# Another opening, and the weighted values of the second half one piece later, in a kernel of two cross-attention layers

## What is computed

```python
q = hidden_state @ Wq + bq                    # 112 x 512
k = encoder_hidden_state @ Wk + bk            # 375 x 128
v = encoder_hidden_state @ Wv + bv            # 375 x 128
...
scores = jnp.einsum('bkgld,bksd->bkgls', q, k) * scale
scores = scores + encoder_attention_mask[:, :, None, :, :]
attn = jax.nn.softmax(scores, axis=-1)
out = jnp.einsum('bkgls,bksd->bkgld', attn, v)
out = out.transpose(0, 3, 1, 2, 4).reshape(b, l, H)
out = out @ Wo + bo
x = out + hidden_state
...
return (x - mu) * jax.lax.rsqrt(var + EPS) * gamma + beta
```

## Time and profile before

| | |
|---|---|
| time before, median of 3 runs | 1741.35 us (1740.72 to 1744.32) |
| the profiled execution's own time | 1738.81 us |
| its span, from the first to the last instruction | 1737.0 us |
| PE busy | 1695.1 us, 98% of the span |
| DVE, ACT, POOL busy | 1267.2, 1042.3, 572.3 us |
| mean granted TensorE clock | 0.990 of full speed |

### The profile page before, as it was taken

The page is one execution under the profiler, slowest core; times in us unless marked ns, Lnnn a source line. Parts: engine busy times, 40 slices in busy tenths (PEclk is TensorE's granted clock), DMA queues, the critical chain, the costliest instruction groups (busy, mean ns, idle before and its releaser), DMA issues. The chain is left out here.

```text
span 1737.0 us, 35992 instructions
## 1 busy us (share of the span) xinstructions
PE 1695.1 (98%) x10881; PEld 1005.9 (58%) x10881; DVE 1267.2 (73%) x1713; ACT 1042.3 (60%) x2370; POOL 572.3 (33%) x1169
## 2 busy tenths in 40 slices
PE   5999999999999999999999999999999999999997
PEld 3555566665565665565665565655665655656652
DVE  5567777787777777777777776777767877767776
ACT  2556666666665656665656665666656666656564
POOL 3133332333332333332333323333323333323332
PEclk8899999999999999999999999999999999999999
DMA  8546555455545465555565454455454455453541
GB/s 283 146 121 170 147 122 143 128 145 143 147 120 142 124 151 145 135 130 147 128 156 145 114 136 130 118 135 145 105 135 125 128 138 139 109 135 115 139 113 55
DMA packets 288390, 235.83 MB, mean 136 GB/s; under 512 B 140858, under 2 KB 262964, under 8 KB 288084
## 3 DMA queue, kind: packets, MB, share of 16 engines
q1 hardware_dynamic: 266852, 204.14, 43.8%
q10 hardware_dynamic: 21488, 31.06, 7.3%
HBM read 101.39 MB, written 22.02 MB: 71 GB/s over the span
## 5 line engine op out<-in xcount | busy, mean ns | idle before, releaser
L922 DVE TENSOR_REDUCE mx<-ms 128x2 f32<-128x750 f32 x896 | 809.2, 924 | 399.0 <-PE ms L1090 392.5
L740 ACT ACTIVATE probs<-sc 125x448 f32<-125x448 f32 x1522 | 744.6, 542 | 281.8 <-PE sc L1061 274.7
L1090 PE MATMUL ms<-ks,qs 96*128 96x375 bf16 (+1 forms) x2560 | 443.0, 327 | 11.4 <-DVE mx L922 8.7
L1061 PE MATMUL sc<-qs,ks 99*125 99x448 bf16 x1522 | 429.2, 358 | 6.0 <-DMA qs<-mT 3.7
L1111 PE MATMUL pv<-probs,vs 125*32 125x448 f32 x3048 | 313.2, 544 | 0.0
L1061 PEld LDWEIGHTS sc<-qs,ks 99*125 99x125 bf16 x1522 | 192.7, 137 | 204.2 <-ACT probs L740 127.8
L1090 PEld LDWEIGHTS ms<-ks,qs 96*128 96x128 bf16 (+1 forms) x2560 | 174.8, 98 | 194.3 <-issue 66.2
L1165 PE MATMUL job<-wo,on 128*112 128x512 f32 x504 | 258.2, 594 | 0.0
L936 DVE RECIPROCAL orec<-osum 128x112 f32<-128x112 f32 x256 | 213.0, 834 | 6.8 <-DMA osum<-oraw 6.8
L1183 PE MATMUL job<-xT,wq 128*128 128x224 f32 x1008 | 214.5, 356 | 0.0
L1134 PEld LDWEIGHTS job<-wv,ctxT 128*125 128x125 f32 x1536 | 191.5, 189 | 16.5 <-issue 0.3
(11 more groups left out here) (70 smaller groups left out, 1034.5 us busy)
## 6 DMA issues: line engine op xcount, KB each, us to landing
ctxT<-in_ctxT SPq DMA_DIRECT2D x64, 750.0 KB, 4.7
qs<-qp SPq DMA_DIRECT2D x756, 56.0 KB, 2.5
ks<-kp SPq DMA_DIRECT2D x765, 46.9 KB, 2.7
osum<-oraw ACTq DMA_DIRECT2D x125, 112.0 KB, 2.9
oc<-oraw ACTq DMA_DIRECT2D x125, 112.0 KB, 3.6
mask<-in_mask SPq DMA_DIRECT2D x64, 164.1 KB, 5.1
xT<-in_xT SPq DMA_DIRECT2D x32, 224.0 KB, 4.6
xin<-in_x SPq DMA_DIRECT2D x32, 224.0 KB, 3.0
```

The source lines that it names most:

```text
L740: nc.scalar.activation(probs[0:KCS, k, j, :], bank[0:KCS, 0:GL], ACT.Exp)\
L922: nc.vector.tensor_reduce(mx[o][:, cols], ms[n % 2][:, :, 0:S2], AX_X, ALU.max).then_inc(max_done[o], 1)
L1061: last = nc.tensor.matmul(bank[0:KCS, 0:GL], ks[p][0:KM, g, rows], qs[p][0:KM, g, :], start=True, stop=not masked)
L1090: last = nc.tensor.matmul(to, qs[o][0:KT, group, cols], ks[o][0:KT, group, :], start=True, stop=not masked)
```

## The change

**Tables.** The weighted values of the second half move from piece 0 to piece 1 of the slot behind in both lines, on PE (`SECOND_HALF_AT`), with ACT's copy; `outputs` for it moves from behind piece 1 to behind piece 2; the first mixed maximum moves from piece 0 to piece 1. The slot (0, 0) has a table row of its own (3), with no maxima in pieces 0 and 1.

**Opening.** All seven pieces of mask bits are issued by SP, ahead of the second context and `Wv`, which now come behind the first terms. PE runs three matmuls on the constant `ident4` before it waits for `Wk` (`keep_clock`), and twelve behind the queries' projection. The second unit's keys and the first unit's values are projected in the slot (1, -1) between the maxima. Two POOL memsets go behind the identity matrices. Weights that are needed later are loaded later and in parts (`weights`), with waits of their own (`rows_in`).

```diff
-BEARLY = 2
+CLOCK = (3, 12)
...
-KEYS_AT = [{2: (0,), 3: (1, 2), 4: (3,)}, {2: (0, 1), 3: (2, 3)}, {0: (0, 1, 2, 3)}]
-VALUES_AT = [{1: (0, 1), 2: (2,)}, {4: (0,), 5: (1,), 6: (2,)}, {0: (0, 1, 2)}]
+KEYS_AT = [{2: (0,), 3: (1, 2), 4: (3,)}, {2: (0, 1), 3: (2, 3)}, {0: (0,), 1: (1,), 2: (2,), 3: (3,)}]
+VALUES_AT = [{1: (0, 1), 2: (2,)}, {4: (0,), 5: (1,), 6: (2,)}, {8: (0,), 9: (1,), 10: (2,)}]
...
-MIXED_AT = [(0, 8), (0, 7), (0, 6)]
+SECOND_HALF_AT = [1, 1, 0, 1]
+MIXED_AT = [(1, 8), (1, 7), (0, 6)]
...
-OUT_AT = [(11, 1), (9, 1)]
+OUT_AT = [(11, 2), (9, 2)]
...
+STEPS_AT[3] = [0, 0, 2, 2, 1, 2, 1, 1, 0, 2, 0, 1]
+MIXED_AT[3] = (2, 8)
+KEYS_AT[3] = {3: (0,), 4: (1, 2), 5: (3,)}
...
 def opening_slot(p):
+    if p == 1:
+        max_rows(0, 0, 1)
     sp.wait_ge(k_p3[p], 1)
     if p == 0:
         stack_terms(0, 0, ks[0], kp[0], 1)
+        stack_terms(0, 1, ks[0], kp[0], 1, of=(1, 2))
         sp.wait_ge(q_p1[0], 2)
         stack_terms(0, 0, qs[0], qp, 0, of=(0,))
-        stack_terms(0, 1, ks[0], kp[0], 1, of=(1, 2))
+        stack_terms(0, 1, ks[0], kp[0], 1, of=(0,))
+        load_ctx(1, 0, 0)
+        load_wv(0, w_v)
         stack_terms(0, 1, qs[0], qp, 0, of=(0,))
         load_mask(0, 0, 0)
     else:
         stack_terms(1, 0, ks[1], kp[1], 1)
         load_ctx(0, 1, 0)
         for u in range(PAR):
             load_xT(u, 1, 0)
-        max_rows(0, 0, 1)
-        load_wo(0, w_in[0])
-        load_rows(0, w_in[0])
+        load_wo(0, w_in[0], slice(0, 2))
...
-load_ctx(1, 0, 0)
-load_wv(0, w_v)
-for n in range(BEARLY, BLOADS):
+for n in range(BLOADS):
     sp.dma_start(mbits[:, BROW * n:BROW * (n + 1)], mbits_d[n]).then_inc(mf_in[n], 16)
...
-    if k == 0 and p_ok:
+    if k == SECOND_HALF_AT[q] and p_ok:
         pv_out(o, 1, post, post + o)
...
-    if k == 0 and p_ok and not last_weighted(p, i):
+    if k == SECOND_HALF_AT[q] and p_ok and not last_weighted(p, i):
         values(o, 1, post)
-    if k == 0:
+    if k == MIXED_AT[q][0]:
         maxima(1)
...
+def keep_clock(times):
+    for _ in range(times):
+        nc.tensor.matmul(ms[0][0:S, 0, 0:GL], ident4[:, 0, :], ident4[:, :, :].rearrange("p c l -> p (c l)"),
+                         start=True, stop=True)
+keep_clock(CLOCK[0])
 pe.wait_ge(w_k, 16 * NK)
-for p in range(PAR):
-    slots(False, opening=True)(p, -1, exists(p, -1), layers(p, -1))
+slots(False)(*FIRST, exists(*FIRST), layers(*FIRST))
+keep_clock(CLOCK[1])
```

More of the change, by code:

```diff
@@ L109, in step_order @@
     return order
-ORDER = [step_order(q) for q in range(PAR + 1)]
+ORDER = [step_order(q) for q in range(len(STEPS_AT))]
 OPENS = [[min(n for at in o for n, h, _, _ in at if h == half) for half in range(2)] for o in ORDER]
@@ L146, in table_row @@
 def table_row(p, i):
-    return 2 if first_values(p, i) else p
+    return 2 if first_values(p, i) else 3 if isinstance(i, int) and (p, i) == (0, 0) else p
 def opens(p, i):
@@ L156, in first_outputs, with first_rows @@
 def first_outputs(p, i):
-    return isinstance(i, int) and (p, i) == (1, 0)
+    return isinstance(i, int) and (p, i) in ((1, 0), (1, PER))
+def first_rows(p, i):
+    return isinstance(i, int) and (p, i) == (0, 1)
 def last_scores(p, i):
@@ L289, in cross_attention_two_layers @@
         w_in = two(sem, "w_in")
+        rows_in = two(sem, "rows_in")
         mf_in = [sem(f"mf_in{n}") for n in range(BLOADS)]
@@ L650, in residual_rows @@
                 def residual_rows():
+                    if first_outputs(p, i) and i == 0:
+                        pool.wait_ge(w_in[0], 16 * NW[0])
+                    if first_outputs(p, i) and i == PER:
+                        pool.wait_ge(rows_in[1], 16 * NR[1])
                     pool.wait_ge(x_in[o], 16 * (post + 1))
@@ L871, in slot @@
                             cast_rests(h)
-                    if opens(p, i) and k == SEND_QUERIES_AT:
+                    if opens(p, i) and k == SEND_QUERIES_AT[0]:
                         act.wait_ge(q_p1[p], 2)
+                        send(0, qs[p], qp, 0, (0,))
+                    if opens(p, i) and k == SEND_QUERIES_AT[1]:
                         act.wait_ge(q_p2[p], 2)
                         act.wait_ge(q_p3[p], 2)
-                        send(0, qs[p], qp, 0, range(PARTS))
-            for n in range(BEARLY):
-                act.dma_start(mbits[:, BROW * n:BROW * (n + 1)], mbits_d[n]).then_inc(mf_in[n], 16)
+                        send(0, qs[p], qp, 0, (1, 2))
             act.wait_ge(warm_set, 1)
@@ L1016, in slot @@
                             reciprocal(k - RECIPROCALS_AT[p])
+                if first_outputs(p, i) and i == PER:
+                    dve.wait_ge(rows_in[1], 16 * NR[1])
             run(dve, slot)
@@ L1022, in _, with slots @@
         def _(pe):
-            def slots(masked, opening=False):
+            def slots(masked):
                 def slot(p, i, has, lay):
@@ L1029, in slot @@
                     q = table_row(p, i)
-                    projects = opening or not opens(p, i)
-                    if first_outputs(p, i):
-                        pe.wait_ge(w_in[0], 16 * NW[0])
                     if starts_layer(p, i):
@@ L1037, in slot @@
                     job_free = [(o_evac[p], stored + 1) if s_ok else (mt_evac[p], 2 * main + 1) if m_ok else None]
-                    if first_values(p, i):
-                        job_free[0] = (q_evac, NG // 2) if opening else (v_ready[o], 1)
+                    if isinstance(i, int) and (p, i) == (0, 0):
+                        job_free[0] = (v_ready[p], 1)
                     def take_job_bank():
@@ L1129, in project_values @@
                             take_job_bank()
-                        if first_values(p, i):
+                        if 0 in chunks and first_values(p, i):
                             pe.wait_ge(w_v, 16 * NV)
@@ L1163, in project_outputs @@
                             pe.wait_ge(on_ready[u], 2 * n + heads[0] // 2 + 1)
+                        if 0 in heads:
+                            if first_outputs(p, i) and i == 0:
+                                pe.wait_ge(w_in[0], 16 * NW[0])
+                            if first_outputs(p, i) and i == PER:
+                                pe.wait_ge(rows_in[1], 16 * NR[1])
                         for c in heads:
@@ L1217, in maxima @@
                         def maxima(part):
-                            for n, half, tiles, place in ORDER[q][k] if a_ok and not opening else ():
+                            for n, half, tiles, place in ORDER[q][k] if a_ok else ():
                                 if place == part:
                                     maximum(n, half, tiles, place)
-                        if k == 0 and a_ok and masked and not opening:
+                        if k == 0 and a_ok and masked:
                             pe.wait_ge(mask_in[o], 16 * (ahead + 1))
-                        if k == PIECES - 1 and a_ok and not masked and not opening:
+                        if k == PIECES - 1 and a_ok and not masked:
                             pe.wait_ge(mask_in[o], 16 * (ahead + 1))
@@ L1246, in slot @@
                             maxima(1)
-                        if k == COLUMNS_AT[q][0] and a_ok and not opening:
+                        if k == COLUMNS_AT[q][0] and a_ok:
                             max_columns(o, 0, ahead)
```

83 lines of the change are left out of this document (43 added, 40 removed).

## The result

| | before | changed |
|---|---|---|
| median | 1741.77 us (1740.72 to 1744.32, 4 runs) | 1757.64 us (1755.5 to 1760.6, 4 runs) |
| profiled execution, its span | 1738.81, 1737.0 us | 1759.49, 1757.6 us |

The account below looks back on a forecast made before the run. Behind the opening PE's instruction stream was taken as the bound, so added waits lengthen the kernel. Steady slots +22.5 us and opening -10.2 us gave +12.3 us, forecast 1753.5 us, range 1740 to 1762.

Parts of the forecast that it names:

- Even slots: Steady even slots, second scores pair: PE waits 0.55 us for exponentials, taken as 0.58, in 31 slots: 18 us.
- Odd slots: Steady odd slots, second scores pair, mostly covered by an output-projection head: wait 0.17 us, taken as 0.15, 30 slots: 4.5 us.
- The steady sum: All slots behind the opening: the added PE waits cost +22.5 us, the rest of the new order costed at nothing.
- (a) The flag: Opening, up to the first maxima: 1.06 MB less moved ahead saves 2.7 us, between 0 and 4.
- (b) Slots (1, -1) and (0, 0): Opening: projections fit PE's gaps, full clock saves 3.4 us, late terms and closer scores cost: -1 us, +3 to -3.
- the first rival: Opening: second context lands after the first maxima, PE stands, clock falls; -3 us instead of -10.2, 1761 us; chance 0.14.
- (c) Slot (1, 0): Opening's last slot: wait for rows of maxima and low clock go, closer scores cost 0.9: -6.5 us, -3 to -8.
- The opening's sum: All opening steps together: -10.2 us, between 0 and -15.
- my main case: Whole kernel: steady slots +18 to +24, opening -7 to -15, so 1745 to 1758 us; chance 0.62.
- The rule that I weighed: Steady slots: weight-load share shows PE has room, so the wait might vanish, 0 instead of +22.5 us; given little weight.
- rival 2: Faster: the wait at the slot's start is absorbed by later waits, steady slots cost 0, 1731 us; chance 0.12.
- rival 3: Same: the steady wait is only half as long, 11 us, which the opening pays, 1742 us; chance 0.12.

Follow-up runs that it names:

- run 5: Changed kernel, with a third of the second half's weighted values (8 of 24 matmuls) left in piece 0: 1748.16 us, ratio 1.0045.
- run 8: Changed kernel, with one whole maximum of piece 1 put in piece 0, in even and odd slots: 1761.12 us, ratio 1.0129.
- run 4: Kernel before, with the move of weighted values and mixed maximum in odd slots alone: 1750.37 us, one run.
- run 6: Changed kernel, with the first mixed maximum kept in piece 0 and only the values in piece 1: 1763.48 us, ratio 1.0134.
- run 7: Changed kernel, with all weighted values and outputs back in their old pieces, only the mixed maximum in piece 1: 1748.18 us, ratio 1.0051.
- run 9: Changed kernel without the move of values, mixed maximum and outputs, and without the matmuls on a constant: 1731.22 us, ratio 0.9951.
- run 10: Changed kernel without the move, with seven second-layer loads issued at the end of slot (0, 0) as in the kernel before: 1736.93 us, ratio 0.9984.
- run 1: Changed kernel with weighted values, first mixed maximum and outputs back in their old pieces, the new opening alone: 1731.58 us, ratio 0.9949.

## Why the prediction was right

The mechanism and the size of the steady part were right. The opening gave about half of what I forecast, and that the total still came within 4 us is in part luck.

**Even slots**: predicted 1.66 us to the next instruction and a wait of 0.55; measured 1.67 and 0.56; I took 0.58. Runs 5 and 8 show that cover is what it lacks. **Odd slots**: predicted 0.17, taken as 0.15; measured 0.20 in the first layer, both in the profile and in run 4. **The steady sum**: 0.58 + 0.15 = 0.73 us per pair predicted, 0.83 and 0.76 measured in the two layers; for all slots behind the opening +22.5 predicted, +23.1 in 29 pairs and 0.7 in the slot (0, 1) ahead of them.

**Missing in it**: I costed the new order of the rest at nothing. The values' projection now stands behind the mixed maximum and takes 1.85 us instead of 1.75, while scores behind it no longer take 0.05 us more: +0.06 us per pair, 2 us. It is small only because the change took the mixed maximum along. Runs 6 and 7 show that to part it from the values costs 0.3 us per slot.

**(a) The flag**: -2.7 predicted, -3.7 in this profile. In the eight other profiles of this opening it was -1.6 to -3.8. That leaving the constant matmuls out does not change the time (run 9) agrees with its reason, that they fill a wait.

**(b) Slots (1, -1) and (0, 0)**: this step failed. -1 predicted, +2.5 measured (29.90 to 73.57 is 43.67 us, against 41.20 before). I left the slot (1, -1) at its old length, with the projections in PE's gaps; it takes 16.6 us instead of 13.2. The second unit's keys wait 1.64 us for their context, loaded later, and the projections then start at the lower clock (1.46 us for two matmuls, which take 0.80 later on), so that VectorE, which was busy nearly without a pause here before, now stands idle for 2.71 and 0.93 us in front of two reduces. The slot (0, 0) runs at the upper clock, as forecast, but is only 1.0 us shorter, not 3.4: waits of 0.44 us for an exponential and of 0.80 us for a reduce now stand in its first pieces, and the rest was not taken apart. I named a clock at 0.50 behind the flag as what would make the step fall, and it stood there until 37.3 us. So the late context of the first rival came true; together with the low clock it cost 3.4 us in the slot (1, -1). The low clock is not shown to come from it: the clock had fallen at 30.5 us, ahead of the wait for the context. All nine profiles of this opening have that wait, of 1.0 to 2.7 us, and a slot (1, -1) of 15.8 to 18.1 us.

**(c) Slot (1, 0)**: -6.5 predicted, -4.2 measured. The cause was right: run 10 brings the wait for rows of maxima back, and 5.4 us, with the seven loads alone. With the move left out (run 1) the slot takes 24.26 us, 7.5 less than before, somewhat more than forecast. What was mis-sized is the +0.9 for the two scores pairs that now stand close: it is 3.3 us, a wait of 1.08 us and the low clock that comes with it (24.26 against 27.58 us). Most of this wait could have been priced from the kernel before. There ACT starts the exponentials of this slot's first scores 1.23 us behind them (76.07 against 74.84), since it issues two transfers first, and it does so in the changed kernel (74.80 against 73.57). By the same sum as for the other slots, an estimate, the next instruction follows at 1.23 + 0.98 + 0.29 = 2.50 us; measured were 2.68 (73.57 to 76.25). The first line is of the kernel before, the second of the changed one:

```profile
76.07 0.98 ACT L740 ACTIVATE probs<-sc 125x448 f32<-125x448 f32 x2 [0.94 <-PE sc L1061]
```

```profile
74.80 0.98 ACT L766 ACTIVATE probs<-sc 125x448 f32<-125x448 f32 x2 [0.94 <-PE sc L1084]
```

**The opening's sum**: -10.2 predicted, -5.5 measured up to the start of the slot (0, 1), -5.2 with the move left out (run 1). That is inside the range of 0 to -15 that I gave it, but outside the -7 to -15 of my main case, between it and the -3 of the first rival.

**The total**: between the two profiled executions the difference is 20.6 us, where +12.3 was forecast. The opening gave 4.7 us less than forecast, the slots behind it cost 1.3 more, and the end 2.2 more. The medians differ by 15.9 us only, since the profiled execution of the kernel before was 3.0 us faster than its median, and that of the changed kernel 1.9 us slower than its own. All three errors have one sign, and the medians show about half of them.

**The marker** that I named, 15 to 20 us of idle time in the matmul line, did not come (3.0 us). The even slot's first two scores pairs did stand 1.0 us apart, and the first maxima came at 29.9 us, near 31; but the slot (0, 1) started at 101.2 us, not near 96. Waits for an exponential as short as these lie in PE's busy time and in the weight load's waits. The busy share could therefore not tell this wait from work. The rule that I weighed (the Trainium skill, Perfetto Trace Analysis, Identifying the Most-Contended Engine) takes the share of the weight loads, beside one of useful arithmetic, as the measure of headroom. That a wait would then vanish was my own inference from it, and it would have given 0 for the steady part; the runs give +23.1. PEld's share was 58% before and is 57% in the kernel that is 20.6 us longer, so it told nothing of this wait.

**Rivals**: 2 and 3 are excluded by the pair's 53.27 us. Nothing was given back later in the slot. For rival 2 I spread the 8.7 us of waits for reduces over all pairs, 0.28 us each; in the steady part it is one wait of 0.17 to 0.18 us per pair, and the rest stands in the opening and at the end.

## What to carry to other kernels

On an engine whose stream is full, look at what stands between the first read of a double-buffered bank and its next write: a group of other work there is cover, and it can be priced from rows before it is moved (start of the reader, its length, the step behind it). Cover is not free to cut up: a group of narrow matmuls that is split in two paid for its passages again here, so try to move such neighbours together. Price a cover in every kind of slot where the edit applies: where ACT was late with other work, in the slot (1, 0), the same move cost 3.3 us and not 0.2. When a change has two parts with opposite signs, run each alone: here the opening, 7.9 us faster, was hidden under a move that costs some 24 us on top of it, and the best version was the change with the move left out, 1731.6 us.

## What the runs showed of the hardware

- Going from matmuls with 112 to 128 output rows to ones with 32 and back cost 0.30 us per extra round in an even slot (run 7, 6.31 against 6.01 us), with the same instructions and no wait for an exponential in it. In run 5 it was about 0.1 us on the way in (0.41 to 0.42 instead of 0.32 us), and 0.05 to 0.13 on the way out, which the last narrow or the first wide matmul carries.
- In the changed kernel a wait of 0.3 us for a semaphore appears as longer matmuls in the records, and not as idle time: two scores matmuls last 0.84 us where 0.54 is usual, and 0.68 instead of 0.38 us pass from their start to the next instruction.
- A pair of banks came back to PE for the second scores in three steps that can be added up: 0.39 us from the scores' start to the exponential's, 0.98 us for the two exponentials, 0.29 us until PE's next instruction behind the scores. The sum, 1.66 us, was measured at 1.67.
- 15 matmuls on a constant raised the granted clock of the stretch from 10 to 30 us from 0.80 to 1.00, and the kernel's time did not change (1731.2 against 1731.6 us). In both profiles the first maxima wait for a transfer of terms at the end of that stretch, 2.13 us without them and 2.90 with.
